# Token blocks: a unit of the next block's attention moves beside the feed-forward products, the PE loop grows from 4 to 16 blocks, and the gate's second product is made in one split pass

## The chip, the cores and the metric

The kernel runs on one core of a Trainium2 chip. A core has a matrix engine (PE, TensorE), a vector engine (DVE), a scalar engine for activations (ACT), a general engine (POOL, GpSimd) and a sync engine (SP) that issues DMAs here. Each runs its own instruction stream, and the streams meet by semaphores only. The metric is the device time of one execution in microseconds (us).

## What is computed

```python
x = x + attn(layernorm(x))       # 2 x 8192 tokens of 512 features, 16 heads of 32
x = x + ffn(layernorm(x))
# attn, in chunks of 64 tokens
q, k, v = proj(x, Wq), proj(x, Wk), proj(x, Wv)
gate  = sigmoid(silu(x @ Wg1 + bg1) @ Wg2 + bg2)      # hidden width 16
alpha = 0.9 * gate + 0.1
intra = softmax(causal(q @ k.T / sqrt(32))) @ v       # within a chunk
inter_t = q_t @ S;  S = alpha_t * S + k_t v_t         # a state over all tokens
out = inter + intra
# ffn: 8 of 64 experts by router, at most 256 tokens each, plus a shared expert
shared = silu(x @ Wsg) * (x @ Wsu) @ Wsd
```

## The kernel before

The program has two parts. `phase_tokens` takes the 16,384 tokens in 64 blocks of 256 and does all but the routed experts. `phase_experts` follows it and is not touched. Products of full precision are split: every operand is held as a high part (fp32r) and a low part, and three passes are made (`split_product`, L727 to L729). The gate's second product (`gate2`, L760) is the exception: it takes plain fp32 operands `wg2` and `s1`.

All orders are written out by hand, one list of calls for each engine, in a loop over blocks. In the round of block t the PE does attention of block t (four units u = 0 to 3, each half the heads of half the tokens), projections for block n = t+1, and then the shared expert of t:

- A unit is `scores(t,u)` (L828, L842), masking and row maxima on DVE (`softmax_a`, L1169 to L1173), `exp` on ACT (L589, eight pieces), division on DVE (`softmax_b`), `turn_probs` on PE (L864), `weights` on DVE (L1192, `WT`), `outputs` on PE (L886, L898), `ot` on ACT (L597).
- `scores` needs `QD` and `KD`, which POOL makes of the decays (`unpair`, `fold`, `decayed_k`, `decayed_q`). `state` on DVE carries the state `S` over chunks and makes `R` for `outputs`.
- The gate for block n: `gate1` on PE (L727 to L729 with `wg1`), tanh and bias on ACT (L554, L555), the product of both on DVE (`silu1`, L1107, writes `s1`), `gate2` on PE (L760), tanh on ACT, `decays` on DVE.
- `turn_out`, `residual`, `norm2`, `x2t` (L919), `router` (L929, L933) and `turn_logits` lead to the shared expert: `gate_up` in three parts, `down` in three. `state_updates` (L808) stands between the parts of `down`, and `positions` (L951, L952) last. `xt` (L742) turns the normalised input `XN` of block t+2, which `normalise` on ACT (L539) writes.

`outputs(t,0)` waits for `pos_used` of block t-1, which `route_c`, the last DVE operation of a round (L1251, L1252), gives. `x2t` on ACT (L605, writes `XTh`) waits for `v_filled` of block n, since the products of `values` read the same tile. The PE list is unrolled over 4 blocks, so its loop has 16 rounds; those of DVE, ACT and POOL are unrolled over 2 blocks. Four PSUM banks are shared by name (`BANK_OF`): `take` makes a job wait until the one before it in its bank is read.

Of the kernel before, what the change touches and what calls it, by code (L numbers as in the profile page):

```python
# [32 lines left out]
GH = 16  # L33
GP = 128
# [18 lines left out]
GB = 4  # L53

# [10 lines left out]
BANK_OF = {"G1": 3, "Qa": 0, "G2a": 2, "G2b": 3, "Ka": 0, "Qb": 1, "Kb": 2, "ATr0": 3, "V0": 0, "V1": 1, "ATr1": 2,  # L65
           "X2Ta": 3, "X2Tb": 0, "KTok0": 2, "RL": 1, "KTok1": 3, "GU0": 2, "RLT": 1, "GU1": 0, "GU2": 3, "DK": 1,
           "DN0": 2, "DN1": 0}
JOBS = list(BANK_OF)
PROJECT = ["G1", "Qa", "G2a", "Qb", "G2b", "Ka", "Kb", "V0", "V1", "KTok0", "KTok1", "DK"]
# [51 lines left out]
def phase_tokens(nc, x_rows, Wq, bq, Wk, bk, Wv, bv, Wg1, bg1, Wg2, bg2, router_w, ws_gate_up,  # L121
                 ws_down, out_rows, norm_rows, counts_dram, ends_dram):
    ctx = ExitStack()
    with ctx:
# [19 lines left out]
        wg2 = sb("wg2", [GP, DIM])  # L144
# [22 lines left out]
        s1 = sb("s1", [GP, TB])  # L167
        AL = sb("AL", [P, KC, NS * PAD])
# [84 lines left out]
        g1_tanh = event("g1_tanh", 2)  # L253
        s1_ready = event("s1_ready")
# [90 lines left out]

        wg1_f = XR[:, 1, 0:KC * GP].rearrange("p (c n) -> p c n", c=KC)
        rw = XR[0:E, 0, 0:DIM]
        staged.append((wg1_f, wg1[0][:, :, :], wg1[1][:, :, :], None))
        WEIGHT_DMAS = 8
# [6 lines left out]
        def _(sp):  # L356
# [8 lines left out]
            sp.dma_start(wg1_f[:, :, 0:GH], Wg1.rearrange("(c p) n -> p c n", p=P)).then_inc(weights_in, 16)  # L365
            sp.dma_start(wg2[0:GH, :], Wg2).then_inc(weights_in, 16)
# [3 lines left out]
            sp.dma_start(b1[0:GH, :], bg1.rearrange("(p o) -> p o", o=1)).then_inc(weights_in, 16)  # L370
# [35 lines left out]
        def _(pool):  # L406
# [11 lines left out]
            nc.gpsimd.memset(wg2[:, :], 0.0)  # L418
# [114 lines left out]
        def _(act):  # L533
# [117 lines left out]
            act.wait_ge(w_low, len(staged) + 1)  # L651
# [3 lines left out]
            gate1(t)  # L655
            q_evac(t, 0)
# [8 lines left out]
            act.wait_ge(v_filled.sem, t.value(v_filled))  # L665
            normalise(t.next())
            xt_evac(t.next())
            with act.Fori(0, NBLK // 2) as pair:
                for odd in range(2):
                    t = Turn(pair, odd)  # L670
                    n = t.next()
                    exp(t, 0)
                    gate1(n)
                    q_evac(n, 0)
# [3 lines left out]
                    exp(t, 1)  # L678
                    ot(t, 0)
                    k_evac(n, 0)  # L680
                    exp(t, 2)
                    q_evac(n, 1)
                    ot(t, 1)
                    exp(t, 3)
                    k_evac(n, 1)
                    ot(t, 2)
                    ot(t, 3)
                    x2t(t)
                    ktok_evac(n, 0)
                    lt(t)  # L690
                    ktok_evac(n, 1)
                    gu(t, 0)
                    hidden_high(t, 0)
                    normalise(t.next(2))
                    router_exp(t)
                    gu(t, 1)
                    hidden_high(t, 1)
                    gu(t, 2)
                    hidden_high(t, 2)
                    xt_evac(t.next(2))  # L700
# [3 lines left out]
        def _(pe):  # L704
# [31 lines left out]
            def xt(t, k):  # L736

                b = XT_BANK[k]
                pe.wait_ge(xn_ready.sem, t.value(xn_ready))
                for a in range(2):  # L740
# [13 lines left out]
            def gate2(t, k, jobs=JOBS):  # L754
# [58 lines left out]
            def scores(t, u):  # L813
# [31 lines left out]
                if u == 0:  # L845
                    pe.wait_ge(qd_ready.sem, t.value(qd_ready))
                    pe.wait_ge(kd_ready.sem, t.value(kd_ready))
                    pe.wait_ge(xl_ready.sem, t.next().value(xl_ready, 0))
# [129 lines left out]
            pe.wait_ge(rw_ready, 4)  # L978
            pe.wait_ge(w_low, len(staged) + 1)
            first = Turn(0, 0)  # L980
            for k in range(2):
                xt(first, k)
# [14 lines left out]
            for odd in range(2):  # L997
                state_updates(first, odd, PROJECT)
            for k in range(2):
                xt(first.next(), k)  # L1000
            with nc.Fori(0, NBLK // 2, 2, engines=[pe.engine], hint_back_edge=True) as pair:
                for odd in range(4):
                    t = Turn(pair, odd)


                    scores(t, 0)
                    gate1(t)
                    project(t, 0, wq, q_filled, ("Qa", "Qb"))
                    scores(t, 1)
                    gate2(t, 0)  # L1010
                    gate2(t, 1)
                    turn_probs(t, 0)
                    project(t, 0, wk, k_filled, ("Ka", "Kb"), parts=(0,))
                    outputs(t, 0)
                    project(t, 0, wk, k_filled, ("Ka", "Kb"), parts=(1,))
                    scores(t, 2)
                    project(t, 1, wq, q_filled, ("Qa", "Qb"), parts=(0,))
                    turn_probs(t, 1)
                    project(t, 1, wq, q_filled, ("Qa", "Qb"), parts=(1,))
                    outputs(t, 1)  # L1020
                    project(t, 1, wk, k_filled, ("Ka", "Kb"), parts=(0,))
                    scores(t, 3)
                    turn_out(t, 0)
                    values(t, 0, chunks=(0,))
                    turn_probs(t, 2)
                    project(t, 1, wk, k_filled, ("Ka", "Kb"), parts=(1,))
                    outputs(t, 2)
                    values(t, 0, chunks=(1,))
                    turn_probs(t, 3)
                    values(t, 0, chunks=(2,))  # L1030
                    outputs(t, 3)
                    values(t, 0, chunks=(3,))
                    turn_out(t, 1)
                    values(t, 1, chunks=(0, 1))
                    x2t(t, 0)
                    values(t, 1, chunks=(2, 3))
                    x2t(t, 1)
                    ktok(t, 0)
                    router(t)
                    ktok(t, 1)  # L1040
                    gate_up(t, 0)
                    turn_logits(t)
                    gate_up(t, 1)
                    xt(t.next(2), 0)
                    xt(t.next(2), 1)
                    gate_up(t, 2)
                    down(t, 0, (0, 1))
                    state_updates(t, 0)
                    down(t, 1, (0, 1))
# [760 lines left out]
```

## Time and profile before

| | |
|---|---|
| median of 3 runs | 4704.45 us (4701.52 to 4705.84) |
| the profiled execution | 4707.31 us, its span 4705.4 us |
| busy share of the span | PE 95%, DVE 75%, ACT 48%, POOL 28% |
| mean granted TensorE clock | 0.982 of full speed |
| idle time of POOL before L475, by DVE L1125 | 2540.0 us in 65 waits |
| idle time of DVE before L1169, by PE L828 | 185.3 us in 144 waits |

Idle time of an engine that is not the bottleneck costs nothing. The PE's busy time covers overlapping, pipelined instructions, so the pitch of starts is read rather than the duration of one.

### The profile page before, as it was taken

How to read it: one execution, taken by the hardware profiler on the slowest of the kernel's cores; microseconds unless marked ns; L12 is line 12 of the kernel's file. 1: busy time of each engine (PE TensorE's matmuls, PEld its weight loads, DVE VectorE, ACT ScalarE, POOL GpSimd, SP SyncE). 2: the span in 40 equal slices, each digit the busy share in tenths (PEclk: the TensorE clock that was granted, in tenths of full speed). 3: DMA queues.
4: the chain of work that ended last, by engine and by line, in shares of the span. 5: the costliest groups of instructions: out<-in, count | busy, mean ns of one | idle time of the engine just before them, and what ended most of it. 6: DMA issues, size and time to landing. Idle time of an engine off the chain costs nothing. (4 is left out here: it accounts for less than half of the span.)

```text
span 4705.4 us, 183217 instructions
## 1 busy us (share of the span) xinstructions
PE 4477.3 (95%) x74416; PEld 3897.4 (83%) x74416; DVE 3518.8 (75%) x7639; ACT 2271.9 (48%) x7475; POOL 1334.0 (28%) x1275
## 2 busy tenths in 40 slices
PE   6999999999999999999999999999999969999998
PEld 5888888888888888888888888888888859999998
DVE  5777777777777777777777777777777768888887
ACT  4444444444444444444444444444444436666665
POOL 2111111111111111111112121211111146666666
PEclk9999999999999999999999999999999979999999
DMA  2000000101000000000000000001000069999997
GB/s 66 31 31 31 31 31 31 36 31 36 28 34 31 31 31 31 31 31 31 31 31 31 31 31 31 31 31 35 31 31 31 31 207 268 270 268 265 267 271 193
DMA packets 195054, 358.52 MB, mean 76 GB/s; under 512 B 16736, under 2 KB 92896, under 8 KB 194352
## 3 DMA queue, kind: packets, MB, share of 16 engines
q1 hardware_dynamic: 160848, 269.47, 16.9%
q0 software_dynamic: 33632, 79.73, 7.8%
q8 instruction: 564, 9.24, 0.8%
q14 instruction: 10, 0.08, 0.0%
HBM read 243.87 MB, written 107.50 MB: 75 GB/s over the span
## 5 line engine op out<-in xcount | busy, mean ns | idle before, releaser
L589 ACT ACTIVATE PR<-PR,MX 128x64 f32<-128x64 f32 x2048 | 682.6, 335 | 811.6 <-DVE MX L1171 811.6
L475 POOL TENSOR_TENSOR RI<-PV,AL 128x512 f32<-128x512 f32 x65 | 78.5, 1208 | 2540.0 <-DVE PV L1125 2540.0
L727 PE MATMUL bank<-XTh,wsguh 128*128 128x256 f32 x1536 | 447.0, 291 | 0.0
L1663 PE MATMUL ebank<-XH,WH 128*128 128x256 f32 x1536 | 431.2, 281 | 6.8 <-DVE XL L1745 6.8
L728 PE MATMUL bank<-XTl,wsguh 128*128 128x256 f32 x1536 | 430.4, 280 | 0.0
L729 PE MATMUL bank<-XTh,wsgul 128*128 128x256 f32 x1536 | 430.4, 280 | 0.0
L1663 PE MATMUL ebank<-XH,WL 128*128 128x256 f32 x1536 | 429.7, 280 | 0.0
L1663 PE MATMUL ebank<-XL,WH 128*128 128x256 f32 x1536 | 429.5, 280 | 0.0
L589 ACT ACTIVATION_READ_ACCUMULATOR PR<-PR,MX 128x1 f32 x2048 | 383.0, 187 | 0.0
L1738 DVE TENSOR_TENSOR WL<-WS,WH 128x768 fp32r<-128x768 f32 (+1 forms) x455 | 370.5, 838 | 16.2
L1600 ACT ACTIVATE WH<-WS 128x768 fp32r<-128x768 f32 (+1 forms) x455 | 325.3, 747 | 26.3 <-DMA WS<-in_L_ffn_w_down_dram 26.3
L1169 DVE TENSOR_TENSOR PR<-sa,causal 128x512 f32<-128x512 f32 x256 | 177.0, 692 | 191.1 <-PE sa L828 185.3
L727 PE MATMUL bank<-XTh,wkh 128*128 128x256 f32 x1040 | 315.5, 303 | 0.0
L727 PE MATMUL bank<-XTh,wqh 128*128 128x256 f32 x1040 | 309.9, 298 | 0.0
L1663 PEld LDWEIGHTS ebank<-XH,WH 128*128 128x128 f32 x1536 | 289.2, 188 | 9.6 <-issue 7.2
L728 PE MATMUL bank<-XTl,wqh 128*128 128x256 f32 x1040 | 296.9, 286 | 0.0
L729 PE MATMUL bank<-XTh,wql 128*128 128x256 f32 x1040 | 296.1, 285 | 0.0
L728 PE MATMUL bank<-XTl,wkh 128*128 128x256 f32 x1040 | 291.3, 280 | 0.0
L729 PE MATMUL bank<-XTh,wkl 128*128 128x256 f32 x1040 | 291.1, 280 | 0.0
L1663 PEld LDWEIGHTS ebank<-XL,WH 128*128 128x128 f32 x1536 | 288.2, 188 | 2.5
L728 PEld LDWEIGHTS bank<-XTl,wsguh 128*128 128x128 f32 x1536 | 290.1, 189 | 0.0
L1663 PEld LDWEIGHTS ebank<-XH,WL 128*128 128x128 f32 x1536 | 289.7, 189 | 0.0
(228 smaller groups left out, 13456.6 us busy)
## 6 DMA issues: line engine op xcount, KB each, us to landing
WS<-in_L_ffn_w_gate_dram SPq DMA_DIRECT2D x65, 768.0 KB
WS<-in_L_ffn_w_up_dram SPq DMA_DIRECT2D x65, 768.0 KB
WS<-in_L_ffn_w_down_dram SPq DMA_DIRECT2D x65, 768.0 KB
norm_rows<-XR SPq DMA_DIRECT2D x64, 576.0 KB, 3.1
X<-in_L_attn_x_dram SPq DMA_DIRECT2D x66, 512.0 KB, 3.6
out_dram<-X SPq DMA_DIRECT2D x64, 512.0 KB, 2.9
CR<-token_counts,count_at POOLq DMA_INDIRECT x136
XG<-norm_rows,row_at POOLq DMA_INDIRECT x132, 6.4
```

The lines of the kernel that those rows point to most:

```text
L475: nc.gpsimd.tensor_tensor(inverse[:, :, 0:half], PV[:, :, :], running[:, :, HC:half:-1], ALU.mult).then_inc(folded.sem, 1)
L589: ins = nc.scalar.activation(PR[b][:, j, :], PR[b][:, j, :], ACT.Exp, bias=MX[b][:, j:j + 1], scale=1.0, accum_out=SU[b][:, j:j + 1])
L727: nc.tensor.matmul(out, sh, mh, start=first, stop=False)
L728: nc.tensor.matmul(out, sh, ml, start=False, stop=False)
L729: return nc.tensor.matmul(out, sl, mh, start=False, stop=last)
L1169: link(v.tensor_tensor(PR[b][:, :, :].rearrange("p (x n) k -> p x n k", x=2), sa[:, :, S_COLS].rearrange("p x (n k) -> p x n k", k=C), mas ...
L1600: nc.scalar.activation(WH[t.buf][:, cols], WS[t.buf][:, cols], ACT.Copy).then_inc(wh_ready.sem, 1)
L1663: last = nc.tensor.matmul(bank[HID[m]][:, a * CAP:(a + 1) * CAP], w, x[odd][:, c, :], start=(c == 0 and i == 0), stop=(c == KC - 1 and i = ...
L1738: v.tensor_tensor(WL[t.buf][:, cols], WS[t.buf][:, cols], WH[t.buf][:, cols].bitcast(f32), ALU.subtract).then_inc(wl_ready.sem, 1)
```

## The change

```diff
+COPIES = (0, 32, 64)
+PE_BODY = 16
+PE_LOOPED = (NBLK - 1) // PE_BODY * PE_BODY
...
-        wg2 = sb("wg2", [GP, DIM])
+        wg2 = sb("wg2", [GP, DIM], f32r)
+        sg = sb("sg", [GP, TB], f32r)
...
-            sp.dma_start(wg1_f[:, :, 0:GH], Wg1.rearrange("(c p) n -> p c n", p=P)).then_inc(weights_in, 16)
-            sp.dma_start(wg2[0:GH, :], Wg2).then_inc(weights_in, 16)
+            for at in COPIES:
+                sp.dma_start(wg1_f[:, :, at:at + GH], Wg1.rearrange("(c p) n -> p c n", p=P)).then_inc(weights_in, 16)
+                sp.dma_start(wg2_f[at:at + GH, :], Wg2).then_inc(weights_in, 16)
+                sp.dma_start(b1[at:at + GH, :], bg1.rearrange("(p o) -> p o", o=1)).then_inc(weights_in, 16)
...
# POOL
+                    rstd2(t, 0)
                     unpair(t.next())
+                    rstd2(t, 1)
                     fold(t.next())
                     decayed_k(t.next())
-                    rstd2(t, 0)
                     decayed_q(t.next())
-                    rstd2(t, 1)
                     rstd1(t.next(2))
# ACT
+            def s1_high(t):
+                act.wait_ge(s1_made.sem, t.value(s1_made))
+                act.wait_ge(g2_filled.sem, t.value(g2_filled, back=1))
+                nc.scalar.activation(sg[:, :], s1[:, :], ACT.Copy).then_inc(s1h_ready.sem, 1)
...
                     gu(t, 0)
                     hidden_high(t, 0)
+                    exp(n, 0)
                     normalise(t.next(2))
...
# PE
-                    last = nc.tensor.matmul(b[:, a * TB:(a + 1) * TB], wg2[:, m * P:(m + 1) * P], s1[:, :], start=True, stop=True)
+                    last = nc.tensor.matmul(b[:, a * TB:(a + 1) * TB], wg2[:, m * P:(m + 1) * P], sg[:, :], start=True, stop=True)
...
+            def attend(t):
+                scores(t, 1)
+                gate1(t)
+                outputs(t, 0)
+                project(t, 0, wq, q_filled, ("Qa", "Qb"))
+                gate2(t, 0)
+                gate2(t, 1)
+                turn_probs(t, 1)
+                scores(t, 2)
...
+                x2t(t, 0)
+                values(t, 1, chunks=(0, 1, 2))
+                x2t(t, 1)
+                values(t, 1, chunks=(3,))
+                router(t)
+            def feed(t):
+                n = t.next()
+                gate_up(t, 0)
+                scores(n, 0)
+                turn_logits(t)
+                ktok(t, 0)
+                gate_up(t, 1)
+                ktok(t, 1)
+                xt(t.next(2), 0)
+                xt(t.next(2), 1)
+                gate_up(t, 2)
+                down(t, 0, (0, 1))
+                state_updates(t, 0)
+                down(t, 1, (0, 1))
+                state_updates(t, 1)
+                down(t, 0, (2,))
+                down(t, 1, (2,))
+                turn_probs(n, 0)
+                positions(t)
+            def step(t):
+                feed(t)
+                attend(t.next())
+            attend(first)
+            with nc.Fori(0, PE_LOOPED // 2, PE_BODY // 2, engines=[pe.engine], hint_back_edge=True) as pair:
+                for odd in range(PE_BODY):
+                    step(Turn(pair, odd))
+            for odd in range(PE_LOOPED, NBLK - 1):
+                step(Turn(0, odd))
+            feed(Turn(0, NBLK - 1))
# DVE
+            def s1_low(t):
+                dve.wait_ge(s1h_ready.sem, t.value(s1h_ready))
+                v.tensor_tensor(sg[32:64, :], s1[32:64, :], sg[32:64, :].bitcast(f32), ALU.subtract).then_inc(s1_ready.sem, 1)
...
+                    softmax_a(t, 1)
                     silu1(n)
-                    softmax_a(t, 1)
-                    weights(t, 0)
                     state(t, (2, 3))
+                    s1_low(n)
+                    softmax_b(t, 1)
...
+                    route_rows(t)
+                    weights(n, 0)
+                    state(n, (0, 1))
                     total(t, 0)
                     total(t, 1)
                     route_c(t)
```

`Wg1`, `Wg2` and `bg1` are loaded three times, at rows 0, 32 and 64. `sg` then holds the high part of the gate's hidden values in rows 0 and 64 and the low part in row group 32, and `wg2` the high part of the weights in 0 and 32 and the low part in 64, so one fp32r pass with 128 rows gives the three partial products. It takes an ACT copy (`s1_high`) and a DVE subtraction (`s1_low`) more. The bank table is another one, and 48 of 63 rounds of the PE stand in a loop of three passes; the other 15 are written out behind it.

DVE, the end of a round and the start of the next, before (`X<-bank,X` is `total`, `CT` and `ends` are `route_c`, `PR`, `MX` and `AM` are `softmax_a`, `R` and `U` are `state`):

```order
L1259 TENSOR_TENSOR XTl<-pt_bank,XTh 128x512
L1287 TENSOR_TENSOR X<-bank,X 128x512 x2
L1251 REGISTER_ALU
L1251 TENSOR_SCALAR CT<-ot_bank,ends 64x256
L1252 ISA
L1252 TENSOR_TENSOR ends<-ot_bank,ends 64x1
L1163 REGISTER_ALU
L1169 TENSOR_TENSOR PR<-sa,causal 128x512
```

and in the changed kernel, where `WT` is `weights` of the next block's unit 0:

```order
L1282 TENSOR_TENSOR XR<-PW,rre 128x2x64
L1230 TENSOR_TENSOR WT<-pt_bank,AM 128x512
L1184 ISA
L1184 SCALAR_TENSOR_TENSOR R<-S,keep,FS 128x128
L1188 TENSOR_TENSOR U<-R,bank 128x128
L1100 REGISTER_ALU
L1195 TENSOR_TENSOR R<-U,FX 128x128
...
L1327 TENSOR_TENSOR X<-bank,X 128x512 x2
L1291 ISA
L1291 TENSOR_SCALAR CT<-ot_bank,ends 64x256
L1292 REGISTER_ALU
L1292 TENSOR_TENSOR ends<-ot_bank,ends 64x1
L1207 TENSOR_TENSOR PR<-sa,causal 128x512
```

`weights` and the first half of `state` now stand between the feed-forward work and `total` with `route_c`; the first mask of the round behind them is that of unit 1.

ACT, beside the shared expert, before (`TG` is the tanh of `gu`, `HTh` is `hidden_high`, `XN` is `normalise`, `PB` is `router_exp`):

```order
L629 ACTIVATE TG<-bank 128x256
L612 ACTIVATE HTh<-WG 128x256
L536 REGISTER_ALU
L539 ACTIVATE XN<-X,sh,rs 128x512 x2
L621 ACTIVATE PB<-LG 128x128
L624 REGISTER_ALU
L629 ACTIVATE TG<-bank 128x256
```

and in the changed kernel (`PR,SU` is `exp`, `KTok` is `ktok_evac`):

```order
L641 ACTIVATE TG<-bank 128x256
L624 ACTIVATE HTh<-WG 128x256
L599 REGISTER_ALU
L601 ACTIVATE PR,SU<-PR,MX 128x64 x8
L543 REGISTER_ALU
L546 ACTIVATE XN<-X,sh,rs 128x512 x2
L594 ACTIVATE KTok<-bank 128x512
L636 REGISTER_ALU
L641 ACTIVATE TG<-bank 128x256
```

The eight pieces of `exp(n,0)` now stand ahead of `normalise`.

## Rows read from the trace of the kernel before

**Rows 1.** Windows: busy us by engine, granted PE clock, DMA share, GB/s.
```profile
1000.00:2000.00 1000.00, 965.76 (x18314) 824.56 (x18322) 731.66 (x1639) 451.04 (x1725) 189.57 (x170) 0.98 0.09 31
1002.00:1007.00 5.00, 5.00 (x36) 4.83 (x23) 3.67 (x10) 3.11 (x18) 0.00 (x0) 0.50 0.02 3
1061.00:1066.00 5.00, 5.00 (x82) 4.77 (x84) 3.94 (x10) 3.38 (x18) 0.00 (x0) 1.00 0.32 115
```

**Rows 2.** Timeline of PE at a loop's back edge: start, us, instructions, idle before.
```profile
998.15 0.44 PE L828 MATMUL sa<-QD,KD 32*32 32x64 f32 x32 [1.71 <-issue]
...
1000.86 0.38 PE L842 MATMUL sa<-KT,QT 32*64 32x64 f32 x4 [1.88 <-issue]
```

**Rows 3.** Timeline of PE: block 1's and block 64's first gate product.
```profile
75.53 0.58 PE L727 MATMUL bank<-XTh,wg1h 128*128 128x256 f32 x1
...
3719.62 0.39 PE L727 MATMUL bank<-XTh,wg1h 128*128 128x256 f32 x1
```

**Rows 4.** Timeline of PE in a block away from the back edge.
```profile
1059.60 0.44 PE L828 MATMUL sa<-QD,KD 32*32 32x64 f32 x32
...
1060.96 0.39 PE L727 MATMUL bank<-XTh,wg1h 128*128 128x256 f32 x1
...
1062.49 0.28 PE L727 MATMUL bank<-XTh,wqh 128*128 128x256 f32 x1
...
1065.43 0.44 PE L828 MATMUL sa<-QD,KD 32*32 32x64 f32 x32
...
1067.02 1.97 PE L760 MATMUL bank<-s,wg 128*128 128x256 f32 x8 [0.15 <-DVE s L1107]
1068.82 0.60 PE L864 MATMUL pt_bank<-ident,PR 128*128 128x128 f32 x4
...
1070.78 0.43 PE L886 MATMUL ot_bank<-WT,V 64*32 64x64 f32 x16
...
1072.07 0.38 PE L727 MATMUL bank<-XTh,wkh 128*128 128x256 f32 x1
...
1117.50 0.38 PE L727 MATMUL bank<-XTh,wg1h 128*128 128x256 f32 x1
```

**Rows 5.** Timeline of PE around the router's products of that block.
```profile
1096.12 0.66 PE L919 MATMUL bank<-ident,XR 128*128 128x128 f32 x4 [0.17 <-DVE XR L1212]
...
1098.91 0.60 PE L787 MATMUL bank<-ident,KD 128*128 128x128 f32 x4
```

**Rows 6.** Timeline of DVE around that block's start.
```profile
1058.72 1.39 DVE L1287 TENSOR_TENSOR X<-bank,X 128x512 f32<-128x512 f32 x2 [0.48 <-PE bank L729]
...
1060.42 0.14 DVE L1252 TENSOR_TENSOR ends<-ot_bank,ends 64x1 f32 x1
1061.17 0.69 DVE L1169 TENSOR_TENSOR PR<-sa,causal 128x512 f32<-128x512 f32 x1 [0.61 <-PE sa L828]
1061.89 0.69 DVE L1171 TENSOR_REDUCE MX<-PR 128x8 f32<-128x512 f32 x1
...
1063.10 0.34 DVE L1146 SCALAR_TENSOR_TENSOR R<-S,keep,FS 128x128 f32<-128x128 f32 x1
...
1064.44 0.29 DVE L1157 TENSOR_TENSOR R<-U,FX 128x128 f32<-128x128 f32 x1
...
1069.46 0.69 DVE L1192 TENSOR_TENSOR WT<-pt_bank,AM 128x512 f32<-128x512 f32 x1 [0.44 <-PE pt_bank L864]
```

**Rows 7.** Timeline of ACT: exp, the gate's tanh, XTh, normalise.
```profile
1062.62 0.35 ACT L589 ACTIVATE PR<-PR,MX 128x64 f32<-128x64 f32 x1 [5.21 <-DVE MX L1171]
...
1065.29 0.45 ACT L554 ACTIVATE t<-bank,b1h 128x256 f32<-128x256 f32 x1
...
1096.65 0.60 ACT L605 ACTIVATE XTh<-bank 128x512 fp32r<-128x512 f32 x1 [4.82 <-PE bank L919]
...
1104.05 1.51 ACT L539 ACTIVATE XN<-X,sh,rs 128x512 f32<-128x512 f32 x2
```

**Rows 8.** Timeline of SP's queue while weights are loaded.
```profile
20.69 1.41 SPq L366 DMA_DIRECT2D wg<-in_L_attn_Wg_dram  x1
```

More of the change, by code:

```diff
@@ L253, in phase_tokens @@
         g1_tanh = event("g1_tanh", 2)
+        s1_made = event("s1_made")
+        s1h_ready = event("s1h_ready")
         s1_ready = event("s1_ready")
@@ L638, in _ @@
             nc.scalar.activation(rwT[:, :, 0:E], bank[0][:, 0:KC * E].rearrange("p (a b) -> p a b", a=KC), ACT.Copy).then_inc(rw_ready, 1)
+            nc.scalar.activation(wg2[:, :], wg2_f, ACT.Copy).then_inc(rw_ready, 1)
             nc.scalar.mul(b1h[:, :], b1[:, :], 0.5).then_inc(rw_ready, 1)
@@ L655, in _ @@
             gate1(t)
+            s1_high(t)
             q_evac(t, 0)
@@ L665, in _ @@
             act.wait_ge(v_filled.sem, t.value(v_filled))
+            exp(t, 0)
             normalise(t.next())
@@ L671, in _ @@
                     n = t.next()
-                    exp(t, 0)
                     gate1(n)
+                    exp(t, 1)
+                    s1_high(n)
+                    ot(t, 0)
                     q_evac(n, 0)
@@ L734, in _, with xt @@
             ALL = slice(None)
-            def xt(t, k):
+            def xt(t, k, opening=False):
                 b = XT_BANK[k]
                 pe.wait_ge(xn_ready.sem, t.value(xn_ready))
+                if k == 0 and not opening:
+                    pe.wait_ge(a_masked.sem, t.next(-1).value(a_masked, 0))
                 for a in range(2):
@@ L977, in _ @@
             last.then_inc(rw_turned, 1)
-            pe.wait_ge(rw_ready, 4)
-            pe.wait_ge(w_low, len(staged) + 1)
+            pe.wait_ge(rw_ready, 5)
+            pe.wait_ge(w_low, len(staged) + 2)
             first = Turn(0, 0)
             for k in range(2):
-                xt(first, k)
+                xt(first, k, opening=True)
             gate1(first, PROJECT)
@@ L998, in _ @@
                 state_updates(first, odd, PROJECT)
+            scores(first, 0)
             for k in range(2):
                 xt(first.next(), k)
[L1001 to L1049, printed above, removed]
-                    state_updates(t, 1)
-                    down(t, 0, (2,))
-                    down(t, 1, (2,))
-                    positions(t)
@@ new lines, in _ @@
+            turn_probs(first, 0)
+            def attend(t):
[7 more added lines that the diff above has]
+                scores(t, 2)
+                project(t, 0, wk, k_filled, ("Ka", "Kb"), parts=(0,))
+                outputs(t, 1)
+                project(t, 0, wk, k_filled, ("Ka", "Kb"), parts=(1,))
+                scores(t, 3)
+                turn_out(t, 0)
+                turn_probs(t, 2)
+                project(t, 1, wq, q_filled, ("Qa", "Qb"), parts=(0,))
+                outputs(t, 2)
+                project(t, 1, wq, q_filled, ("Qa", "Qb"), parts=(1,))
+                project(t, 1, wk, k_filled, ("Ka", "Kb"), parts=(0,))
+                turn_probs(t, 3)
+                project(t, 1, wk, k_filled, ("Ka", "Kb"), parts=(1,))
+                outputs(t, 3)
+                values(t, 0, chunks=(0, 1))
+                turn_out(t, 1)
+                values(t, 0, chunks=(2, 3))
+                x2t(t, 0)
[3 more added lines that the diff above has]
+                router(t)
@@ L1310, in _ @@
             silu1(t)
+            s1_low(t)
             decays(t)
@@ L1316, in _ @@
                 values(t, k)
+            softmax_a(t, 0)
             norm1(t.next())
             shift1(t.next())
+            softmax_b(t, 0)
             xt_low(t.next())
+            weights(t, 0)
+            state(t, (0, 1))
             START = links[0]
```

73 lines of the change are left out of this document (36 added, 37 removed).

## The prediction

> **What bounds the kernel now.** I began with windows over the middle of the token part: in 1000 us the PE is busy 965.76 us and DVE 731.66, at a granted clock of 0.98 [rows 1]. So the PE sets the pace, and a microsecond is won either by shorter PE work or by a wait of the PE. From block 1's first gate product at 75.53 to block 64's at 3719.62 there are 63 blocks [rows 3], 57.84 us each. A block away from the back edge takes 1117.50 - 1060.96 = 56.54 [rows 4]. The missing 1.30 us a block, 82 us in all, lies at the 15 back edges of the four-block loop, so about 5.5 us an edge. The timeline there shows two waits on "issue", 1.71 and 1.88 us, inside `scores(t,0)` [rows 2], and then a stretch at a granted clock of 0.50 (1.2 instead of 2.4 GHz), where 5 us hold 36 matmuls instead of 82 [rows 1]. The engine had been idle 3.6 us out of some 4.5 before the clock fell.
>
> Inside a clean block the PE still waits. Like groups have like pitches, so a longer pitch is a wait that busy time hides. `scores` takes 1060.96 - 1059.60 = 1.36, but 1.59 ahead of the gate [rows 4]: 0.23 of waiting for `s1`. From `x2t` to the router's end are 2.79 us [rows 5] for about 1.7 us of work: 1.1. With a dozen smaller ones compared in the same way I estimate 2.9 us of waiting a block.
>
> **The gate's product.** Eight records from 1067.02 to 1068.82 [rows 4]: 1.80 us. In one fp32r pass it is four products of 256 columns. The 24 of `project` take 1065.43 - 1062.49 = 2.94 [rows 4], 0.122 each, so 0.49. Saved: 1.31 us a block, if the PE does not wait there. The page "FP8 and Floating Point Precision" of the Trainium skill (TensorE Precision Notes) says that true FP32 makes four passes; by that 1.80 would become 0.45, the same to 0.04.
>
> **The loop.** 48 rounds in 3 passes leave 2 back edges, and the exit may cost what an edge does. Products of 256 columns now stand behind the edge, which use instructions more slowly than `scores`, so the second wait may go, and the clock with it: between 1.7 and 5.5 us for each of 3, against 82 before. I take 6 in all. "Runtime: NRT & Kernel Launch" of the Trainium skill (Instruction fetch mechanics) says that a taken branch outside the fetched window stalls the sequencer, so that unrolling pays; [rows 2] agree. The same rule speaks against the change at another place, the third rival.
>
> **The new order.** Work of the PE in a block becomes 56.54 - 1.31 - 2.9 = 52.3, less 0.2 for two fewer changes from wide to small products: 52.1. What waits come in its place I worked out by walking the four lists with the durations of the rows. Four places matter.
>
> *Start of `attend`.* `turn_probs(n,0)` is the last but one on the PE, and DVE's `weights(n,0)` starts 1069.46 - 1068.82 = 0.64 after it [rows 4, 6], which is just when `attend` starts (time 0 here). Behind `weights` (0.6) DVE must do half of `state` (1063.10 to 1064.44 + 0.29: 1.63) and `total` with `route_c` (1058.72 to 1060.42 + 0.14: 1.84) [rows 6]: free at 4.07. Before, `softmax_a` stood right behind `route_c` and nothing of attention was queued ahead. Only now comes `softmax_a(t,1)`, whose scores were there at 1.5. Its maxima take 1061.89 + 0.69 - 1061.17 = 1.41 [rows 6]: 5.48. `exp` takes 1065.29 - 1062.62 = 2.67 on ACT [rows 7]: 8.2. Behind it in ACT's queue stands the new `s1_high`, then `s1_low` on DVE, about 0.43 each like the tanh of the same size (0.45) [rows 7]: `sg` is ready at 9.2. The PE would be at `gate2` after 1.36 + 1.53 + 1.29 + 3.0 = 7.2 [rows 4]. Wait: 2.0 us, of which 1.3 already falls at `outputs(t,0)`, since this waits for `pos_used` at 4.2. `softmax_b(t,1)` stands behind `s1_low`, so `turn_probs` waits 0.35 more.
>
> *Middle.* `weights(t,3)` stands behind a reciprocal, and `outputs(t,3)` waits some 0.45 (estimate).
>
> *Router.* The last chunk of `values` now stands behind `x2t(t,1)`, and ACT may write `XTh` only when it is done, 1.38 us after `x2t` starts instead of 0.53 (1096.65 - 1096.12) [rows 5, 7]. From ACT's start to the router's end are 2.26 [rows 5, 7], so 3.64 in all for 2.14 of work: 1.5 us of waiting, now uncovered by `ktok`. It is covered in turn by nothing, but POOL's chain to `QD` ends at about the same time, so removing it alone would not help.
>
> *`xt`.* Let `scores(n,0)` start at 0. Scored at 1.5, maxima at 2.95, `exp` until 5.65, then `normalise`, 1.51 [rows 7], so 7.2 with the signal. The PE is at `xt` after 1.36, two thirds of a microsecond for two small groups, 2.94 to 3.04 and 0.36: 5.45. Wait: 1.75. Before, `normalise` had no `exp` ahead of it.
>
> With 0.25 for small ones: 2.0 + 0.35 + 0.45 + 1.5 + 1.75 + 0.25 = 6.3. A block takes 52.1 + 6.3 = 58.4, against 57.84 with all edges: +0.6, 63 times +37 us. So the gains (1.3 edges, 1.3 gate, 2.9 old waits) are eaten by the new waits.
>
> **Opening.** SP issues six more small DMAs, at most 1.41 us each [rows 8]; between 0 (if the last landing is set otherwise) and 8.5, and I take 7, since ACT and PE wait for all. `scores` and `turn_probs` of unit 0 with their softmax stand ahead of the first `gate1` without cover: 0 to 9, I take 5. The expert part is not touched.
>
> **Sum.** 37 + 6 + 7 + 5 = +55 on the profiled execution's 4707.3, 4762; that lies 2.9 above the median, so 4760.
>
> **Rivals.**
>
> 1. *The waits do not open* (faster, 0.34). For it: DVE has 27% to spare [rows 1] and the walk adds chains of estimates, in which one operation that really starts earlier removes a term. With the old 2.9 us of waiting a block is 55.0: 63 x (55.0 - 57.84) = -179, +18: 4543. If `xt` and the router alone were hidden: 58.4 - 3.25 = 55.15, nearly the same, 4553; if one of them, 4660. Against it: each of the two large chains (DVE to `pos_used` and `gate2`, ACT to `xt`) is made of measured durations one behind the other. It decides from waits of 5.4 us downward.
> 2. *Break-even* (0.05): waits of 5.3 to 5.5, 4700.
> 3. *The edge of DVE's loop* (slower still, 0.07). Every second block the DVE list branches just between `route_c` and `softmax_a(t,1)`, which is now on the path; before, DVE waited for the PE there (0.61 us away from the edge [rows 6]). What its edge costs no row shows: nothing, or as much as the PE's first wait, 1.71 [rows 2]. 31 x 1.71 = +53: 4812. This is what the fetch rule of the Trainium skill named above would do at this place, since the DVE loop stays as it was.
> 4. *The clock falls* (slower, 0.05). Idle of 1.3 and 0.7 at the start and 1.75 at `xt` might be enough in each block. At the edge it took 3.6 us close together [rows 2]. At half clock 5 us of products cost 2.7 more (36 of 82 done), 63 times: +170, 4930.
>
> **Chances and range.** The forecast itself (waits of 5.5 to 7.5 us) has 0.49, and its own range is 4710 to 4835. Below 4610 and above 4850 I leave about 0.12 and 0.06, so the range is 4610 to 4850. This kernel's runs tell a change from none at about 0.2%, 9 us. Faster 0.34, same 0.05, slower 0.61.
>
> **What would show it.** `gate2`'s four products at a pitch of 0.12; two or three back edges with "issue" and hardly a stretch at 0.5; idle or a long pitch on the PE ahead of `outputs(t,0)` and `gate2`, released by DVE (`ends`, `sg`), ahead of `xt` by ACT `XN`, and about 3.6 us from `x2t(t,1)` to the router's end; distances of first gate products of 58.4. Wrong if those are under 57.5: then see which of the four waits is missing.

## The result, and the profile after

The changed kernel takes 4774.66 us (median of 4 runs, 4772.50 to 4777.57), the kernel before 4703.43 us (4 runs, 4701.52 to 4705.84). The ratio is 1.0152, with a 95% interval of 1.0136 to 1.0168: 1.5% slower. The forecast was 4760, in a range of 4610 to 4850.

The profiled execution of the changed kernel has a span of 4775.5 us. Busy time by engine from its page, and a window over the middle as in [rows 1]:

```profile
PE 4365.6 (91%) x74256; PEld 3817.3 (80%) x74256; DVE 3504.0 (73%) x7716; ACT 2307.3 (48%) x7557; POOL 1336.8 (28%) x1275
...
1000.00:2000.00 1000.00, 922.01 (x17970) 789.63 (x17968) 717.64 (x1635) 450.75 (x1702) 194.17 (x175) 1.00 0.09 31
```

The PE is busy 922.01 us of 1000 where it was 965.76 [rows 1], and the clock is 1.00 where it was 0.98. So the products did become cheaper and the clock did stop falling, and still the kernel is slower: the PE now idles 78 us of these 1000, where it idled 34. The first gate products of blocks 0, 1, one in the middle, and 64 (the timeline of the PE; in brackets the idle time of the engine just ahead, and what ended it):

```profile
43.56 0.58 PE L743 MATMUL bank<-XTh,wg1h 128*128 128x256 f32 x1 [1.41 <-DVE XTl L1299]
...
89.32 0.58 PE L743 MATMUL bank<-XTh,wg1h 128*128 128x256 f32 x1
...
1144.88 0.38 PE L743 MATMUL bank<-XTh,wg1h 128*128 128x256 f32 x1
...
3781.35 0.38 PE L743 MATMUL bank<-XTh,wg1h 128*128 128x256 f32 x1
```

Blocks 1 to 64 take 3781.35 - 89.32 = 3692.0, against 3644.1 [rows 3]: +48 us, 58.60 a block for 57.84. Block 1 begins 13.8 us later (89.32 for 75.53). Behind block 64's first gate product stand 4775.5 - 3781.35 = 994.2 us, before 4705.4 - 3719.62 = 985.8: +8.4. Together 70.1, which is the whole difference of the spans.

Where the PE waits, by what releases it (total, times, longest; from 100 to 3800 us):

```profile
PE sa L760 <- ACT XN L546: 95.0, 63, 1.6
PE ot_bank L905 <- DVE ends L1292: 60.0, 63, 1.1
PE bank L948 <- ACT XTh L617: 51.5, 63, 0.9
PE ot_bank L905 <- DVE WT L1230: 24.8, 63, 0.4
PE bank L778 <- DVE sg L1145: 24.3, 62, 0.5
PE pt_bank L883 <- DVE PR L1220: 19.7, 120, 0.2
PE sa L860 <- issue: 1.9, 2, 1.6
```

and the same view of the kernel before, from 100 to 3700 us:

```profile
PE sa L842 <- issue: 31.8, 15, 2.7
PE sa L828 <- issue: 27.3, 23, 1.7
```

This pair tells the story. Before, the long waits came from the loop's edge (59 us on "issue"). Now "issue" is all but gone, and six waits that come in nearly every one of 63 blocks hold 275 us, 4.4 a block. They are `xt` (L760), `outputs(t,0)` (L905 behind `ends`), the router (L948), `outputs(t,3)` (L905 behind `WT`), `gate2` (L778) and `turn_probs` (L883). Most of them at their places, from the end of one round through the next:

```profile
1059.99 0.60 PE L938 MATMUL bank<-ident,XR 128*128 128x128 f32 x4
...
1062.14 0.91 PE L948 MATMUL bank<-XTh,rwT 128*128 128x256 f32 x4 [0.86 <-ACT XTh L617]
1062.89 0.94 PE L952 MATMUL bank<-XTl,rwT 128*64 128x256 f32 x4
1064.24 0.38 PE L743 MATMUL bank<-XTh,wsguh 128*128 128x256 f32 x1 [0.42 <-issue]
...
1067.28 0.44 PE L846 MATMUL sa<-QD,KD 32*32 32x64 f32 x32
...
1072.41 0.60 PE L805 MATMUL bank<-ident,KD 128*128 128x128 f32 x4
1074.53 0.66 PE L760 MATMUL sa<-ident,XN 128*128 128x128 f32 x4 [1.52 <-ACT XN L546]
...
1085.05 0.44 PE L846 MATMUL sa<-QD,KD 32*32 32x64 f32 x32
...
1086.41 0.38 PE L743 MATMUL bank<-XTh,wg1h 128*128 128x256 f32 x1
...
1089.04 0.43 PE L905 MATMUL ot_bank<-WT,V 64*32 64x64 f32 x16 [0.95 <-DVE ends L1292]
...
1090.33 0.38 PE L743 MATMUL bank<-XTh,wqh 128*128 128x256 f32 x1
...
1093.86 0.72 PE L778 MATMUL bank<-sg,wg 128*128 128x256 f32 x4 [0.42 <-DVE sg L1145]
1094.73 0.66 PE L883 MATMUL pt_bank<-ident,PR 128*128 128x128 f32 x4 [0.15 <-DVE PR L1220]
```

1085.05 is the start of `attend`. The first gate product at 1086.41 and the one at 1144.88 are 58.47 us apart. The "issue" wait of 0.42 at 1064.24 is one of the two back edges. The engines that the PE waits for, at the same places (DVE's `weights(n,0)`, and `ends` with the first mask behind it, then ACT's `exp(n,0)` and `XN`, and POOL's `QD` of the next block):

```profile
1084.88 0.69 DVE L1230 TENSOR_TENSOR WT<-pt_bank,AM 128x512 f32<-128x512 f32 x1 [1.35 <-PE pt_bank L883]
...
1088.63 0.14 DVE L1292 TENSOR_TENSOR ends<-ot_bank,ends 64x1 f32 x1
1088.70 0.67 DVE L1207 TENSOR_TENSOR PR<-sa,causal 128x512 f32<-128x512 f32 x1
```

```profile
1070.30 0.35 ACT L601 ACTIVATE PR<-PR,MX 128x64 f32<-128x64 f32 x1 [1.00 <-DVE MX L1209]
...
1072.97 1.50 ACT L546 ACTIVATE XN<-X,sh,rs 128x512 f32<-128x512 f32 x2
...
1122.88 2.20 POOL L509 TENSOR_TENSOR QD<-QT,AL 128x1024 f32<-128x1024 f32 x1
```

DVE does `weights(n,0)`, half of `state`, `total` and `route_c` without a gap from 1084.88 to 1088.7, and only then is free for unit 1. ACT begins `XN` behind the last piece of `exp(n,0)`.

### The profile page after: what moved, and what is told of

Read it like the earlier page. It is cut to its first block and busy times, and to the rows that moved or that the text cites. A ratio compares the mean times of both kernels' runs of the same rounds, so it can differ in the third digit from the quotient of the medians.

```text
span 4775.5 us, 183033 instructions
## 1 busy us (share of the span) xinstructions
PE 4365.6 (91%) x74256; PEld 3817.3 (80%) x74256; DVE 3504.0 (73%) x7716; ACT 2307.3 (48%) x7557; POOL 1336.8 (28%) x1275
## 5 line engine op out<-in xcount | busy, mean ns | idle before, releaser
L462 POOL TENSOR_TENSOR rs<-ve,neg_half 128x1 f32<-128x1 f32 x128 | 69.2, 540 | 2700.6 <-DVE ve L1243 2700.6
L743 PE MATMUL bank<-XTh,wsguh 128*128 128x256 f32 x1536 | 441.7, 288 | 0.9 <-issue 0.8
L1230 DVE TENSOR_TENSOR WT<-pt_bank,AM 128x512 f32<-128x512 f32 x257 | 177.8, 692 | 187.9 <-PE pt_bank L883 139.8
L743 PE MATMUL bank<-XTh,wqh 128*128 128x256 f32 x1040 | 311.1, 299 | 0.0
L743 PE MATMUL bank<-XTh,wkh 128*128 128x256 f32 x1040 | 310.9, 299 | 0.2 <-issue 0.2
L1315 DVE SCALAR_TENSOR_TENSOR WG<-TG,bank 128x256 f32<-128x256 f32 x192 | 80.4, 419 | 305.6 <-ACT TG L641 305.6
L905 PE MATMUL ot_bank<-WT,V 64*32 64x64 f32 x8192 | 220.3, 222 | 85.4 <-DVE ends L1292 60.0
L743 PEld LDWEIGHTS bank<-XTh,wsguh 128*128 128x128 f32 x1536 | 289.5, 188 | 1.8 <-issue 1.6
```

The costliest lines, as they stand in the source:

```text
L462: nc.gpsimd.tensor_tensor(rs2[:, k:k + 1], ve2[:, k:k + 1], neg_half[:, k:k + 1], ALU.pow).then_inc(rstd2_ready.sem, 1)
L743: nc.tensor.matmul(out, sh, mh, start=first, stop=False)
L905: last = nc.tensor.matmul(ot_bank[D * r:D * r + D, col:col + C], V[rows, tile, h * D:(h + 1) * D], WT[u % 2][rows, pair, C * (r % 2):C * ( ...
L1230: v.tensor_tensor(WT[u % 2][:, :, :], pt_bank[:, :].rearrange("p (n k) -> p n k", k=P), AM[u % 2][:, :, :], ALU.add).then_inc(w_ready.sem, 1)
L1315: link(v.scalar_tensor_tensor(WG[:, :], TG[:, :], 1.0, b[:, 0:TB], ALU.add, ALU.mult))
```

## The experiments

Ratios are to the kernel before, measured beside each on the same chip. The kernel before had medians of 4702.36 to 4704.95 us beside the experiments, so a difference between two of the other kernels is good to some 3 us only. Where it is 7 to 11 us, the 95% intervals of the two ratios overlap, and the distances of first gate products in the two traces are given beside it.

**1 and 2. `totals_first` and `norm_first`: one long wait each.** On DVE both `total` go ahead of `weights(n,0)`, and `route_c` ahead of `state`:

```diff
                     route_rows(t)
-                    weights(n, 0)
-                    state(n, (0, 1))
                     total(t, 0)
                     total(t, 1)
+                    weights(n, 0)
                     route_c(t)
+                    state(n, (0, 1))
```

> The changed kernel with one edit: on DVE both `total` stand ahead of `weights(n,0)`, and `route_c` ahead of `state(n,(0,1))`. Theory (the new waits are set by what is queued on DVE and ACT): `route_c` ends some 2 us sooner, so `outputs(t,0)` no longer waits, and `softmax_a(t,1)` starts about 0.8 us sooner after the start of `attend`, so `gate2` too. A block 0.8 us shorter, 63 times -50: about 4725 us. Rival (the PE's own products and their changes set the block): no change, 4775.

Measured: 4742.38 us (4739.15 to 4743.35), 1.0080 [1.0063, 1.0097]. That is 32 us under the change as it was.

In the other kernel `normalise` goes ahead of `exp` on ACT, with the DVE operation that feeds it:

```diff
# ACT
-                    exp(n, 0)
                     normalise(t.next(2))
+                    exp(n, 0)
# DVE
+                    shift1(t.next(2))
                     softmax_a(n, 0)
                     hidden_low(t, 0)
-                    shift1(t.next(2))
```

> The changed kernel with one edit: `normalise(t+2)` stands ahead of `exp(n,0)` on ACT, and `shift1` ahead of `softmax_a(n,0)` on DVE, as it needs. Theory: the wait of 1.5 to 1.75 us at `xt` goes; `exp(n,0)` comes 0.5 us later and may give 0.4 to 0.7 back at the third `gate_up` (KTok0 is read later) or at the last `down`. 1.0 to 1.75 us a block, 63 to 110 in all: 4665 to 4712 us. Rival (the time lost at `xt` is only the slack of a longer chain through DVE, such as the last `hidden_low`): it comes back in full behind it, 4775.

Measured: 4683.95 us (4683.53 to 4685.37), 0.9958 [0.9941, 0.9975]: 91 us less, and under the kernel before. `XN` now starts at 1044.76 and is done before the PE comes for it. The PE in `norm_first`, where `xt` follows `ktok` with no wait:

```profile
1047.97 0.60 PE L805 MATMUL bank<-ident,KD 128*128 128x128 f32 x4
1048.40 0.60 PE L760 MATMUL sa<-ident,XN 128*128 128x128 f32 x4
```

The pitch is 0.43 where it was 2.12: 1.69 less in each block, of which 1.44 arrive at the end of it (91 over 63). In `totals_first` the wait behind `ends` is gone from the list, but another has grown (waits of the PE, 100 to 3700 us):

```profile
PE bank L778 <- DVE sg L1145: 34.2, 54, 1.2
```

`gate2` waits 34.2 us for `sg` where it was 24.3: the wait partly passes to the next product that needs DVE. Still most blocks come near the 0.8 us of the expectation: the distances of first gate products are 57.44 and 57.97 in turn (medians) where they were 58.4, 46 us over 63 blocks, and 6 us more are gained behind the last one. What is missing from the 50 stands in few blocks. In the rounds around the two edges of the PE's loop and its exit `totals_first` is 18.4 us above its typical blocks, the changed kernel 4.9. The second of these places in `totals_first`, a wait of the PE and a window right behind it:

```profile
1957.26 0.58 PE L744 MATMUL bank<-XTl,wkh 128*128 128x256 f32 x1 [1.19 <-issue]
...
1957.00:1970.00 13.00, 12.74 (x196) 11.32 (x197) 5.84 (x13) 3.99 (x19) 0.00 (x0) 0.50 0.01 3
```

The wait stands some 30 us ahead of the branch, and the granted clock is at 0.50 behind it. The changed kernel has neither there. Why the same loop does this in one order and not in the other was not tested.

**3. `both_orders`: do the waits form one chain?** Both edits.

> The changed kernel with both edits of the two orders. Theory: the two waits lie in different halves of the block and add up, -1.8 to -2.5 us a block, 4617 to 4662 us, below the kernel before (4703). Rival (one chain that runs round the block): no more than the larger of the two alone.

Measured: 4649.58 us (4647.04 to 4651.40), 0.9883 [0.9867, 0.9900]. The gain is 125 us, and 32 + 91 = 123. The two waits add up, in typical blocks too: 0.74 us and 1.44 us a block alone, 2.09 together. They are two chains, each set within its own stretch of the round.

**4. `before_loop16`: the loop alone.** The kernel before with 16 blocks in the PE's loop.

```diff
-            with nc.Fori(0, NBLK // 2, 2, engines=[pe.engine], hint_back_edge=True) as pair:
-                for odd in range(4):
+            with nc.Fori(0, NBLK // 2, 8, engines=[pe.engine], hint_back_edge=True) as pair:
+                for odd in range(16):
```

> The kernel before with the PE's loop over 16 blocks instead of 4 and nothing else: 3 back edges instead of 15. Theory (5.5 us an edge, by waits on instructions and the clock that falls after them): 12 x 5.5 = -66, 4637 us, and stretches of granted clock 0.5 only at the 3 edges left. Rival (the clock falls by a period of its own, since its stretches stand 232 us apart): only the idle part of an edge goes, 12 x 3.7 = -45 at most, 4659, and the clock still falls every 232 us.

Measured: 4628.07 us (4627.97 to 4629.47), 0.9840 [0.9824, 0.9857]. 12 fewer edges give 74 us, 6.2 each. At an edge that is left, and in a window right behind it and one of 700 us without an edge:

```profile
978.08 0.44 PE L828 MATMUL sa<-QD,KD 32*32 32x64 f32 x32 [2.23 <-issue]
...
981.36 0.79 PE L842 MATMUL sa<-KT,QT 32*64 32x64 f32 x17 [2.45 <-issue]
...
982.00:987.00 5.00, 5.00 (x61) 4.75 (x57) 3.39 (x8) 2.60 (x16) 0.00 (x0) 0.62 0.01 3
2000.00:2700.00 700.00, 686.93 (x13353) 585.81 (x13353) 530.54 (x1182) 325.61 (x1251) 134.04 (x120) 1.00 0.09 32
```

The clock falls behind the edge and nowhere else in the stretch (1.00 over 700 us). So the falls of before belong to the edge and do not come on a period of their own.

**5. `after_loop4`: the edge at its new place.** The changed kernel with `PE_BODY = 4`.

```diff
-PE_BODY = 16
+PE_BODY = 4
```

> The changed kernel with the PE's loop over 4 blocks instead of 16 (15 passes, then 3 rounds written out), begun at `gate_up` as in the changed kernel. Theory: what follows the edge decides its price. The 24 wide products of `gate_up` use instructions slowly, and the block has waits that take up part of a late start; the changed kernel's distances of blocks are 0.6 us longer at the edge and 0.7 behind it. 12 edges more at 1.3: +16, 4790 us, and no stretch at a granted clock of 0.5 in the token part. Rival: an edge costs its 5.5 us wherever it stands, +66, 4840 us.

Measured: 4785.78 us (4784.86 to 4788.53), 1.0181 [1.0164, 1.0198]. The 12 more edges cost 11 us: 0.9 each, not 6 (7 us by the distances of first gate products, 58.72 for 58.60). The longest total wait of its PE on "issue", 100 to 3800 us, and a window behind one of the edges:

```profile
PE bank L743 <- issue: 3.7, 14, 0.3
...
2940.50:2943.70 3.20, 3.20 (x17) 3.20 (x17) 1.01 (x4) 0.00 (x0) 1.88 (x2) 0.50 0.00 0
```

14 waits of at most 0.3 us stand at the first product of `gate_up` (L743), against the 59 us inside `scores` before. The expectation of no half clock in the token part was a miss: the granted clock falls to 0.50 behind two of the 14 edges and behind the exit (at 2940, 3176 and 3650 us), where the round takes 60.50 to 62.73 us; around the other edges it takes 58.97 to 59.45.

With the edge ahead of `gate_up`, the loop of 16 is worth 11 us; ahead of `scores` it was worth 74. The two pairs of kernels differ in the place of the edge, and also in the order of the round and in the 4.4 us of waits that can take up a late start. So the place is the likely cause, and not shown alone. The price of that place is not fixed either: the rounds around the two edges and the exit are 4.9 us above typical blocks in the changed kernel, 7.1 in `norm_first`, 11.4 in `after_orders` (experiment 8) and 18.4 in `totals_first`, with the same loop in all; in `before_loop16` it is 20.2 for three edges.

**6 and 7. The gate.** In `after_gate32` the changed kernel makes `gate2` of plain fp32 again, without the extra loads, `s1_high` and `s1_low`.

```diff
-COPIES = (0, 32, 64)
+COPIES = (0,)
...
-                    s1_high(n)
...
-                    last = nc.tensor.matmul(b[:, a * TB:(a + 1) * TB], wg2[:, m * P:(m + 1) * P], sg[:, :], start=True, stop=True)
+                    last = nc.tensor.matmul(b[:, a * TB:(a + 1) * TB], wg2[:, m * P:(m + 1) * P], s1[:, :], start=True, stop=True)
...
-                    s1_low(n)
```

> The changed kernel with the gate's second product in plain fp32 as before: no `s1_high`, no `s1_low`, the weights of the gate loaded once. Theory: the split product saves 1.3 us of the PE, but its input comes 0.9 us later on a path that already waits, so it is worth only about 0.6 us a block here. Without it `gate2` starts when `outputs(t,0)` and `project` are done, about 0.6 us sooner, and takes 1.8 instead of 0.5: +0.6, 63 times +40, less 7 for the opening: about 4808 us. Rival (the PE's work sets the block, so its whole saving counts): +84, 4850 us.

Measured: 4784.96 us (4784.01 to 4786.86), 1.0178 [1.0161, 1.0195]. So the split pass is worth 10 us in this order (12 us in the blocks, 58.79 for 58.60, less what follows on the opening). Its PE in `after_gate32`:

```profile
1093.52 1.89 PE L776 MATMUL bank<-s,wg 128*128 128x256 f32 x8
1095.25 0.60 PE L881 MATMUL pt_bank<-ident,PR 128*128 128x128 f32 x4
```

From `outputs(t,0)` to `turn_probs(t,1)` are 1095.25 - 1089.31 = 5.94 us here and 1094.73 - 1089.04 = 5.69 with the split: 0.25 apart, although the products take 1.73 by pitch instead of 0.72 in the record. The rest is the wait for `sg` and for `PR` behind it. And 2.3 us of the gain are given back in the opening, by the loads: the first gate product of `after_gate32` starts at 41.30, not at 43.56.

`before_loop16_gate` puts the split gate into the old order, with `turn_probs(t,0)` moved ahead of `gate2` to hide the latency:

```diff
# PE
+                    turn_probs(t, 0)
                     gate2(t, 0)
                     gate2(t, 1)
-                    turn_probs(t, 0)
```

> The kernel before with the loop of 16 and the split gate product, and none of the new order (only `turn_probs(t,0)` moved ahead of `gate2`, to use the wait). Theory: `s1_high` and `s1_low` make `sg` 0.9 us later than `s1` was, which is 0.2 us late already, so of 1.3 us some 0.7 are left: 64 times -45, +7 for the opening, from 4628 to 4590 us. Rival (the whole 1.3 counts): -84 + 7, 4551.

Measured: 4635.39 us (4633.01 to 4638.52), 0.9860 [0.9843, 0.9876]: 7 us more than `before_loop16`, where 38 less were expected. Waits of its PE, 100 to 3600 us:

```profile
PE ot_bank L900 <- DVE WT L1210: 55.7, 173, 0.7
PE bank L774 <- DVE sg L1125: 33.9, 60, 0.7
```

In `before_loop16` the same two are 10.3 us (62 times, behind `WT`) and 11.7 us (57 times, behind `s1`). 68 us of waiting are new, 45 at `outputs` and 22 at `gate2`. So the PE's saving turned into waits; `s1_low` and its wait for ACT stand in DVE's queue ahead of `weights`, which would account for those at `outputs`. Of the 7 us, 2.7 are the loads (first gate product at 43.90 for 41.16) and 3 lie in the blocks (56.64 for 56.59).

**8 to 10. The new order with its queues put right.** `after_orders` takes the edits of `norm_first`, and on DVE puts `weights(n,0)` behind `state(n,(0,1))` and both `total`, and `norm2(t,0)` and `weights(t,3)` ahead of both reciprocals (`inverse`):

```diff
                     route_rows(t)
-                    weights(n, 0)
                     state(n, (0, 1))
                     total(t, 0)
                     total(t, 1)
+                    weights(n, 0)
                     route_c(t)
...
                     softmax_b(t, 3)
+                    norm2(t, 0)
+                    weights(t, 3)
                     inverse(n, 0)
-                    weights(t, 3)
                     inverse(n, 1)
-                    norm2(t, 0)
```

> The changed kernel with four moves within the orders: `normalise` ahead of `exp(n,0)` with `shift1` ahead of `softmax_a(n,0)`; `state(n,(0,1))` and both `total` ahead of `weights(n,0)`, in time in which DVE waits; `norm2(t,0)` and `weights(t,3)` ahead of both reciprocals. Theory: against the two edits together (4650) another 0.4 us at the start of `attend` and 0.4 at `outputs(t,3)`: -0.8 a block, 4600 us. Rival (POOL, which waits for the reciprocals, gets late with `QD` and `scores(n,0)` waits for it): the second 0.4 comes back, 4625.

Measured: 4581.09 us (4577.75 to 4584.37), 0.9742 [0.9726, 0.9758]. Waits of its PE, 100 to 3600 us:

```profile
PE bank L948 <- ACT XTh L617: 51.6, 63, 0.9
...
PE bank L778 <- DVE sg L1145: 10.1, 49, 0.3
```

The waits behind `XN`, `ends` and `WT` are gone; the router's is what it was. The kernel is 19 us faster than expected; its four moves were not taken apart.

`orders_gate32` is `after_orders` with the fp32 gate.

> The kernel with the four moves (4581) and the gate's second product in plain fp32. Theory: what the split product is worth depends on how late its input is. Now that `gate2` waits for only some 0.3 us, the PE's own time counts more: 1.75 instead of 0.87 up to `turn_probs`, less the wait, +0.5 us a block, 63 times +32, less 3 for the opening: about 4610 us. Rival (the split is worth nothing wherever it stands, as in the kernel before with the loop of 16, where it cost 7): 4580.

Measured: 4600.18 us (4598.85 to 4603.24), 0.9776 [0.9760, 0.9792]. With DVE no longer late, the split gate is worth 19 us, twice the 10 of experiment 6.

`orders_values_first` is `after_orders` with the four chunks of `values` ahead of `x2t(t,1)`:

```diff
                 x2t(t, 0)
-                values(t, 1, chunks=(0, 1, 2))
+                values(t, 1, chunks=(0, 1, 2, 3))
                 x2t(t, 1)
-                values(t, 1, chunks=(3,))
                 router(t)
```

> The kernel with the four moves (4581), and the last chunk of `values(n,1)` ahead of `x2t(t,1)`, so that ACT no longer waits for `v_filled`. Theory: from `x2t(t,1)` to the router's end runs the chain PE, ACT, DVE of some 2.8 us whatever stands there; the chunk of 0.8 us only moves from under it to ahead of it. Then 0 to -0.1 us a block: 4575 to 4583 us. Rival (the wait on `v_filled` is itself the loss): -0.8 us a block, 4531 us.

Measured: 4564.82 us (4562.33 to 4566.16), 0.9701 [0.9685, 0.9717]: 16 us less: more than the 6 at most of the one theory, and far from the 50 of the other. In it the router waits (timeline of the PE):

```profile
1063.71 0.90 PE L948 MATMUL bank<-XTh,rwT 128*128 128x256 f32 x4 [0.62 <-ACT XTh L617]
```

The gap falls from 0.78 to 0.62 only: `x2t(t,1)` now stands right ahead of the router on the PE, and ACT cannot begin `XTh` before it. This is the fastest kernel of the study, 3.0% under the one before.

## Why the prediction was right, step by step

The mechanism and the main term are right. That the whole came within 15 us is in part the sum of errors with both signs, given below.

**The block.** Forecast 58.4, measured 58.4 in a clean block (most of the 63 lie between 58.41 and 58.46). Mean 58.60: 63 x 0.18, 11.5 us, lie in edges and in some blocks that are longer without one. The rounds around the two edges and the exit take 5.0 us of it (the six distances sum to 355.5 for 6 x 58.42); for these the forecast had 6. The first of the 63 takes 2.1 more.

**The waits.** Those at all four places are there, released by the engines that were named, and in size:

| place | forecast | measured, by pitch |
|---|---|---|
| `xt` | 1.75 | 1074.53 - 1072.41 - 0.36 = 1.76 |
| `outputs(t,0)` | 1.3 | 1089.04 - 1086.41 - 1.53 = 1.10 |
| `gate2` | 0.7 | 1093.86 - 1090.33 - 2.94 = 0.59 |
| `turn_probs` | 0.35 | 0.87 - 0.49 = 0.38 |
| `x2t(t,1)` to the router's end | 3.64 | 1062.89 + 0.75 - 1059.99 = 3.65 |
| `outputs(t,3)` | 0.45 | 0.39 (its gap) |

(0.36 is the pitch of the four `ktok` products, 1.53 and 2.94 those of `gate1` and `project` in [rows 4], 0.75 the pitch from L948 to L952.) `xt` can be followed in full: `exp` starts 3.02 us after `scores(n,0)` (forecast 2.95), and `XN` ends after 7.19 (forecast 7.2). From the start of `attend`, DVE comes to unit 1's mask after 3.65 us (forecast 4.07): its chain takes 3.82 (1088.70 - 1084.88) and began 0.17 ahead. `gate2` starts after 8.81 (forecast 9.2). The walk added durations of [rows 6] and [rows 7] one behind the other, and that is what the queues did.

The six waits (the router's as 3.65 - 2.14 = 1.51) add up to 5.7 us where 6.05 were forecast, and the block came out at 58.4 all the same. So the PE's work and the small waits are 0.3 us more than the 52.1 + 0.25 forecast for them. That the two errors cancel is luck. The step from 58.4 to the sum was loose too: (58.4 - 57.84) x 63 is 35, not 37.

**The gate's product and the clock.** Work was exchanged for waits: busy time per 1000 us falls by 44, and the clock stays at 1.00 through waits of 1.5, 0.95 and 0.85 us in every block, as a window over all whole rounds shows:

```profile
97.00:3841.00 3744.00, 3451.42 (x67402) 2958.26 (x67400) 2690.07 (x6130) 1688.86 (x6380) 715.02 (x640) 1.00 0.09 31
```

The fourth rival (a fall in each block) is refuted. By pitch, `gate2` takes 0.87 with the wait for `PR` behind it, where it took 1.80 [rows 4]; the record of its four products is 0.72 long.

**The edge.** The forecast gave each edge that is left between 1.7 and 5.5 and took 2. By the distances of first gate products, the two edges cost about 1.3 each and the exit about 2.4. The second wait is gone at both edges, as forecast ("issue" 0.42 at a `gate_up` product is left). At the exit one of 1.64 stands inside `scores(n,0)`. Experiment 5 makes the place of the edge the likely reason and rules out the number of edges, but the same loop costs up to 18.4 us for its three places in another order, so the 6 taken here was right for this order only. The Trainium skill ("Runtime: NRT & Kernel Launch", Instruction fetch mechanics) says that a taken branch outside the fetched window stalls the sequencer. The runs agree that it stalls (2.23 and 2.45 us in experiment 4), and show besides that an edge costs 0.9 us ahead of `gate_up` in experiment 5 and 6.2 ahead of `scores` in experiment 4.

**The third rival** (DVE's own edge, +53) did not come: even and odd blocks both take 58.4, and no first mask of DVE waits on "issue". In `totals_first` it does (waits of DVE, 100 to 3700 us):

```profile
DVE PR L1207 <- issue: 14.4, 31, 0.6
```

These are 31 waits of 0.46 us at the first mask of DVE's loop body, one for each of its 31 back edges, and every second distance of the PE is 0.53 longer there (57.97 for 57.44). In `both_orders` the same waits stand, and the blocks alternate between 55.83 and 56.65 us. So the edge of DVE's loop has a price where the PE waits for DVE behind it, 0.5 us and not the 1.71 that the rival took. `after_orders` has no such wait, and why its blocks still alternate (55.19 and 55.45) is open.

**What was mis-sized: opening and expert part.** The sum had 7 + 5 for the opening and nothing behind the token part. Measured: the loads cost 2.5 us (the first gate product at 43.56 for 41.09), not 7. The first block costs 11.3 (45.76 for 34.44), not 5, which is beyond the 0 to 9 given for it. What failed there is the step "stand ahead of the first `gate1` without cover": only the softmax's own time was counted, not who is queued behind it. DVE and PE in the opening:

```profile
76.22 0.69 DVE L1207 TENSOR_TENSOR PR<-sa,causal 128x512 f32<-128x512 f32 x1 [11.54 <-PE sa L846]
...
78.15 1.28 DVE L1119 BATCH_NORM_STATS2 st<-X 128x6 f32<-128x512 f32 x2
...
82.59 1.11 PE L760 MATMUL sa<-ident,XN 128*128 128x128 f32 x4 [6.49 <-ACT XN L546]
```

`softmax_a(t,0)` stands ahead of the normalisation of block 1 on DVE and sits 11.54 us waiting for the scores. So the statistics begin at 78.15, and the PE stands 6.49 us at `xt` with nothing else to do. The whole first block in the changed kernel, then in the kernel before:

```profile
43.50:89.30 45.80, 32.40 (x476) 28.61 (x476) 17.12 (x34) 13.70 (x38) 9.76 (x8) 0.76 0.01 2
...
41.10:75.50 34.40, 30.25 (x380) 27.29 (x380) 13.32 (x21) 10.83 (x21) 9.75 (x8) 0.86 0.01 2
```

The PE idles 13.4 us of it (45.80 - 32.40) where it idled 4.15, so 9.3 of the 11.3 us are idle time. In both kernels the granted clock falls to 0.50 in this block, at 67.1 us behind a wait of 3.2 us, and before at 65.6 behind one of 2.1. It is back at 97.9 us here and at 79.3 before, so the wait of 6.5 us falls into a stretch at half clock; what the longer stretch costs by itself was not taken apart.

Behind the last gate product 8.4 us are lost though the expert code is the same: 3.8 before its first product, 4.5 behind it. They go again when the orders are put right (986.5 us remain in `after_orders`, 4581.0 - 3594.55, against 985.8 before). Most hangs on DVE's order: 987.8 us remain in `totals_first`, 991.8 in `norm_first`. Why the expert part itself runs longer was not tested.

**Sum, as forecast and as measured:** block 37 and 36.5, edges and stray 6 and 11.5, loads 7 and 2.5, first block 5 and 11.3, expert part 0 and 8.4; 55 and 70. The main term is right, and the others missed by -4.5 to +8.4.

**What was wrong in a reason.** For the router the prediction said that POOL's chain to `QD` ends at about the same time, so that removing the router's wait alone would bring nothing. In the changed kernel `QD` ends at 1122.88 + 2.20 = 1125.08, and `scores(n,0)` starts 0.66 us later:

```profile
1125.74 0.44 PE L846 MATMUL sa<-QD,KD 32*32 32x64 f32 x32
```

From the third block on the slack is 0.65 to 0.9 us, but for the two blocks at a back edge. So the reason was half right: POOL's chain would leave room for some 0.7 of the 1.5 us, not for nothing. In `orders_values_first` the slack is 0.43 to 0.53 in nearly every block, and the gain was 0.25 us a block. The router's wait was never removed by itself.

**The first rival** (the waits do not open, 4543 to 4660) was wrong for the change as given. For the order with its queues mended it comes near: `norm_first` gave 4684 where "one of them" alone was put at 4660, and `after_orders` 4581 where 4543 was put for a round without the new waits. It had `xt` and the router together at 4553; no run has just these two.

## What to carry to other kernels

When work of the next iteration is moved up beside this one's, walk every in-order queue it enters: the two longest waits came from an operation placed ahead of a more urgent one (`exp` ahead of `normalise`, `weights` ahead of `total` and `route_c`), and swapping these two back was worth 125 us. Measure a loop's edge in the order that is kept: in front of wide products, in a round with waits, four times the code was worth 11 us, in front of small ones 74. When waits are taken out, look at the edges again, since they took 4.9 us in one order and up to 18.4 in another. A cheaper product pays only as far as its operand is early: the same split gate was worth +19, +10 and -7 us in three orders.

## What the hardware showed that was not expected

- A back edge of the PE's loop costs 6.2 us ahead of `scores` (32-row products; two "issue" waits of 1.8 to 2.5 us, then a clock of 0.62 over 5 us) and 0.9 us ahead of 256-column products in a round with waits. With the same loop of 16 in other orders, the rounds around its two edges and its exit took 4.9 to 18.4 us, and the dearest had "issue" waits of 1.2 us some 30 us ahead of the branch and 10 to 14 us at a clock of 0.50.
- Waits of 1.5 us, with 4.4 us of visible waiting in each 58 us, left the granted clock at 1.00 for 3744 us. Kernels with less waiting did not all keep it: `totals_first`, `both_orders` and `after_orders` have stretches at 0.50 in their token part, most of them near the edges of the PE's loop.
- DVE's own back edge cost 0.46 us in `totals_first` (31 waits, 14.4 us), and nothing visible in the changed kernel.
- Two waits in the same round, one behind ACT and one behind DVE, added up when removed (32 + 91 = 123 for 125 measured).
